# SyncE fetches the rows of the last two batches of each gather pass one by one, in a program without loops

## The chip, the cores and the metric

The kernel runs on one NeuronCore of a Trainium2 chip. The metric is device time in microseconds (us) from start to end of one execution, the median of the executions shown. A core has TensorE (PE; PEld is its weight load), VectorE (DVE), ScalarE (ACT), GpSimd (POOL) and SyncE (SP), each with an instruction stream of its own; they meet through semaphores. SyncE, ScalarE and GpSimd also issue DMAs, which 16 DMA engines carry out.

## What is computed

Four graph layers over 6250 nodes of 128 features and 106250 edges sorted by destination, each followed by a residual and a layernorm:

```
edge_index = stack([src, dst])
x = layernorm(x + L0(x))   # mean over a node's edges of x[src], then concat(x, mean) @ weight
x = layernorm(x + L1(x))   # segment max of relu([h[src], h[dst], w] @ W1 + b1) @ W2 + b2, then a two-layer update
x = layernorm(x + L2(x))   # gated convolution: sigmoid(gelu([x[row], x[col]] @ m1) @ m2) weighs xt[row]
x = layernorm(x + L3(x))   # attention with 4 heads: q[dst] . k[src], softmax over a node's edges, sum of v[src]
```

Every layer needs, for each edge, a row of a table at the edge's source node: `x[src]`, `h[src]` and so on. The number of the row is data, so the rows are gathered.

## The kernel before

Edges are padded to 832 tiles of 128 (`TILES`); four tiles are a batch of 512 edges (`BT`, `BE`), and a pass goes over 208 batches (`BATCHES`). Rows of a tile lie on the 128 partitions. There are four passes with gathers: `edges_sum` (L0, rows of 128 floats), `edges_max` (L1, 128), `edges_gate` (L2a, 192) and `edges_attention` (L3, 256). A fifth pass, `edges_conv` (L2), reads what L2a has put aside and gathers nothing. Between the passes `nodes` works on the nodes.

`gatherer` (L492) is GpSimd's program in a pass: for each batch it waits for a free buffer of eight (`room`, `DEEP`), counts up `s_go`, and issues four indirect DMAs of 128 rows each, whose row numbers stand in `g["src"]` (L503). It is written out without a loop. The other engines run `pipeline` (L63): rounds of 4 or 8 batches (`SLOTS`, `DEEP`) in a hardware loop, with the first and last rounds written out; a stage `(lag, f)` works on the batch that lies `lag` behind. Nothing plans the order: each engine's program is the order.

The data flow of L0: the gathered tiles are turned by TensorE into PSUM (`turn`, L567), VectorE runs a masked running sum over 512 edges (`scan`, L621, which needs the batch's mask), TensorE turns the sums back (L609), ScalarE copies them (L638) and stores them (L629). SyncE loads the masks (`mask_load`, L772, from the table `same`) into four slots, each when the scan four batches before is done, and stores zeros into `seed` (L385). In L1 SyncE loads a seed (L804) and two masks (L772) per batch; TensorE turns the seed (L818), VectorE spreads it over the edges (L855), adds the gathered row (`add_weight`, L846), adds the two (L861) and takes a running maximum (L868); ScalarE's relu and a matmul lie between. In L2a SyncE loads a seed (L925) and a mask (L929); VectorE's spread is L989. In L3 it loads a pair of rows (L1128) and a seed (L1132) per batch, and per four batches two masks (L1137), two rims (L1147) and a store (L1151). In all passes a buffer is given back to GpSimd by the stage that read it.

In a hardware loop, the address of a SyncE DMA follows from the loop's register, by a register operation and a move before the DMA instruction.

Of the kernel before, what the change touches and what calls it, by code (L numbers as in the profile page):

```python
# [13 lines left out]
P = 128  # L14
N, E, D = 6250, 106250, 128
HID = 64
# [11 lines left out]
NSLOTS = 3  # L28
COMBS = 7
# [33 lines left out]
def pipeline(eng, count, slots, stages, first=0):  # L63
# [4 lines left out]
    base, rounds = first // slots, count // slots  # L68
# [76 lines left out]
def build(nc, d, out):  # L145

    with ExitStack() as ctx:
# [12 lines left out]
        g["xT"] = sb("xT", [P, NT * P])  # L160
        g["last"] = sb("last", [P, NT], I32)
# [47 lines left out]
class Setup:  # L209
# [3 lines left out]
    def __init__(self, ph, d, g):  # L213
# [9 lines left out]
         self.s_rim, self.s_open) = (ph.sem(n) for n in ("src", "dst", "w", "x", "same", "id", "mask", "tp", "tc", "slink", "rim", "open"))  # L223
# [28 lines left out]
    def sync_first(self, sp):  # L252
        d, chunk = self.d, lambda a: a.rearrange("(p i) -> p i", p=P)
        sp.dma_start(self.g["src"][:, :], d["src"]).then_inc(self.s_src, 16)
        for j in range(3):
            sp.dma_start(self.dst[j][:, :], chunk(d["dst"][j:j + EP])).then_inc(self.s_dst, 16)
# [230 lines left out]
def edge_buffers(ph, width, depth=DEEP):  # L487
    gath = [ph.sb(f"gath{k}", [P, BT, width]) for k in range(depth)]
    return gath, ph.slot_sems("gath", depth), ph.sem("go")


def gatherer(gp, g, table, gath, s_gath, s_go, s_free, s_copied=None):  # L492

    depth = len(gath)
    for n in range(BATCHES):
        k, r = n % depth, n // depth
        if s_copied:
            stored(gp, s_copied, k, r)
        room(gp, s_free, n, depth)
        gp.sem_inc(s_go, 1)  # L500
        for t in range(BT):
            tile = n * BT + t
            gp.indirect_dma_start(out=gath[k][:, t, :], out_offset=None, in_=table,  # L503
                                  in_offset=bass.IndirectOffsetOnAxis(ap=g["src"][:, tile:tile + 1], axis=0)).then_inc(s_gath[k], 16)
# [17 lines left out]
def edges_sum(nc, d, g):  # L522

    with Phase(nc, "L0") as ph:
        gath, s_gath, s_go = edge_buffers(ph, D)
# [16 lines left out]
        @block.sync  # L542
        def _(sp):
            setup.sync_first(sp)
            beside.sync_before(sp)
            setup.sync_rows(sp)
            load, fill = mask_load(sp, g["same"], mask, s_mask, s_scan), beside.sync_stage(sp)
            pipeline(sp, BATCHES, SLOTS, [(0, load), (0, fill)])
            beside.all_filled(sp)
            setup.sync_last(sp)  # L550

        @block.gpsimd
        def _(gp):
# [3 lines left out]
            gatherer(gp, g, d["x"], gath, s_gath, s_go, s_turn)  # L557

        @block.tensor
        def _(pe):  # L560
            setup.tensor_first(pe, pX)

            def turn(n, k, r):
                landed(pe, s_gath, k, r, BT)
                room(pe, s_scan, n, 2)
                for t in range(BT):
                    m = pe.transpose(pT[k % 2][:, cols(t)], gath[k][:, t, :], g["ident"][:, :])  # L567
# [5 lines left out]
            for first, end, parts in stretches:  # L573
# [5 lines left out]
                pipeline(pe, end, DEEP, [(0, turn), (2, ret)], first=first)  # L579
# [196 lines left out]
def edges_max(nc, d, g):  # L776

    w = g["w"]
    with Phase(nc, "L1") as ph:
        gath, s_gath, s_go = edge_buffers(ph, D)  # L780
# [18 lines left out]
        def _(sp):  # L799
            sp.dma_start(weight[:, :], d["weight"]).then_inc(s_wt, 16)  # L800

            def load_seed(n, k, r):
                room(sp, s_turns, n, SLOTS)
                sp.dma_start(seed[k][:, :].rearrange("p (t f) -> p t f", t=BT), seeds[:, bass.ds(n * BT, BT), :]).then_inc(s_seed[k], 16)  # L804
            pipeline(sp, BATCHES, SLOTS, [(0, load_seed), (0, mask_load(sp, g["same"], same, s_same, s_dest)),
                                          (2, mask_load(sp, g["fresh"], fresh, s_fresh, s_max))])

        @block.gpsimd
        def _(gp):
            gatherer(gp, g, g["tab"], gath, s_gath, s_go, s_sent)  # L810
# [30 lines left out]
        def _(v):  # L841
            def add_weight(n, k, r):
                landed(v, s_gath, k, r, BT)
                room(v, s_turn, n, SLOTS)
                for t in range(BT):
                    a = v.scalar_tensor_tensor(sent[k % SLOTS][:, cols(t)], g["wide"]["W1w"][:, :], weight[:, bass.ds(n * BT + t, 1)],  # L846
                                               gath[k][:, t, :], ALU.mult, ALU.add)
# [22 lines left out]
            pipeline(v, BATCHES, DEEP, [(0, on_short(spread)), (0, add_weight), (1, on_short(add_dest)), (3, on_short(top))])  # L870
# [17 lines left out]
def edges_gate(nc, g, ew):  # L888
# [5 lines left out]
    with Phase(nc, "L2a") as ph:  # L894
        gath, s_gath, s_go = edge_buffers(ph, W2)
# [26 lines left out]
        def _(sp):  # L922
# [7 lines left out]
            pipeline(sp, BATCHES, SLOTS, [(0, load_seed), (0, load_same)])  # L930

        @block.gpsimd
        def _(gp):
            gp.iota(row_i[:, :], [[1, P]], base=0, channel_multiplier=0).then_inc(s_iota, 1)
            gatherer(gp, g, g["tab_h"], gath, s_gath, s_go, s_turn, s_aside)

        @block.tensor
        def _(pe):
            def turn(n, k, r):
# [7 lines left out]
                landed(pe, s_gath, k, r, BT)  # L947
                room(pe, s_pre, n, 2)
                pe.sem_inc(s_tgo, 1)
                for t in range(BT):  # L950
                    m = pe.transpose(pA[k % 2][H, cols(t)], gath[k][:, t, H], g["ident"][:, :])
# [17 lines left out]
            pipeline(pe, BATCHES, DEEP, [(0, turn), (2, dot), (9, count)])  # L969
# [68 lines left out]
        def _(act):  # L1038
# [5 lines left out]
            def put_aside(n, k, r):  # L1044
                landed(act, s_gath, k, r, BT)
                act.dma_start(aside[:, bass.ds(n * BT, BT), :], gath[k][:, :, HID:W2]).then_inc(s_aside[k], 16)
# [5 lines left out]
            pipeline(act, BATCHES, DEEP, [(0, put_aside), (0, on_short(gelu)), (4, on_groups(gate))])  # L1052
# [18 lines left out]
def edges_attention(nc, d, g):  # L1071
# [7 lines left out]
    with Phase(nc, "L3") as ph:  # L1079
        gath, s_gath, s_go = edge_buffers(ph, 2 * D)  # L1080
# [37 lines left out]
        def _(sp):  # L1118
# [33 lines left out]
            pipeline(sp, BATCHES, DEEP, [(0, on_short(load_pair)), (0, on_short(load_seed)), (0, on_groups(load_masks)), (12, on_groups(load_rims)), (19, on_groups(store_fix))])  # L1152
# [4 lines left out]
        def _(gp):  # L1157
# [7 lines left out]
            gatherer(gp, g, g["tab_kv"], gath, s_gath, s_go, s_pv)  # L1165
# [66 lines left out]
        def _(v):  # L1232
# [31 lines left out]
            def times_key(n, k, r):  # L1264
                need(v, s_query, n)
                landed(v, s_gath, k, r, BT)
                v.tensor_tensor(tiled(prod[k % 2][:, :]), tiled(pQ[k % 2][:, :]), gath[k][:, :, 0:D], ALU.mult).then_inc(s_prod, 1)
# [21 lines left out]
            def weigh(n, k, r):  # L1289
                need(v, s_probe, r * rings + k // SLOTS)  # L1290
                landed(v, s_gath, k, r, BT)
# [4 lines left out]
                                gath[k][:, :, D:2 * D].rearrange("p t (h c) -> p t h c", h=HEADS), ALU.mult).then_inc(s_pv, 1)  # L1296
# [544 lines left out]
```

## Time and profile before

| | |
|---|---|
| median of 3 runs (lowest, highest) | 6658.26 us (6647.23, 6663.53) |
| the profiled execution: its time, its span | 6670.73 us, 6669.0 us |
| granted TensorE clock, mean of the span | 0.64 |
| POOL, PE, DVE, ACT busy | 59%, 53%, 52%, 24% of the span |
| first to last gather of L0, L1, L2a, L3 | 5 to 1265, 1450 to 2826, 3028 to 4296, 5033 to 6502 us |

All views below are of that one execution. Times in them are microseconds from the span's start, durations of single instructions in a source view nanoseconds. "SPq" and "ACTq" are instructions of SyncE's and ScalarE's sequencers, DMA issues among them, which do not count as busy. In brackets stands how long the engine was idle before a row and what ended it: "issue" is nothing that the profile shows, "remote" a signal whose sender the profile doesn't name.

### The profile page before, as it was taken

What the parts mean: (1) busy time and instruction counts of PE and PEld (TensorE: products, weight loads), DVE (VectorE), ACT (ScalarE), POOL (GpSimd) and SP (SyncE); (2) the same over time, 40 slices, a digit from 0 to 9 for tenths busy, and PEclk for the clock granted to TensorE, in tenths of its full rate; (3) what the DMA queues carried; (4) which work ended last, traced back from release to release, by engine and by line L of the source; (5) the groups of instructions that cost most, each with busy time, mean ns of one, the idle gap of its engine ahead of it and who ended that gap; (6) DMA issues with size and microseconds to landing.
All of it is one profiled execution on the core that took longest, in us unless ns stands there. A gap on an engine that the chain in (4) does not pass through costs nothing. (4 is left out here: it accounts for less than half of the span.)

```text
span 6669.0 us, 85454 instructions
## 1 busy us (share of the span) xinstructions
PE 3561.5 (53%) x19032; PEld 2752.0 (41%) x19032; DVE 3479.4 (52%) x6921; ACT 1575.8 (24%) x3699; POOL 3955.5 (59%) x4526
## 2 busy tenths in 40 slices
PE   3433332245455555554667676766644676666661
PEld 2222222233333333333555555656633555555451
DVE  4444222225566666653666666778854444444445
ACT  1011000131111111131222222267740111111115
POOL 6666556655565655546666666488865555555552
PEclk6565565567777777775555555588876656666665
DMA  5555445424555555524555555489944555545552
GB/s 172 160 157 153 136 150 154 131 82 145 153 162 154 162 156 155 158 80 123 140 138 142 139 140 138 122 262 290 289 140 140 155 152 150 154 150 152 149 152 54
DMA packets 804105, 1015.40 MB, mean 152 GB/s; under 512 B 230791, under 2 KB 509457, under 8 KB 803988
## 3 DMA queue, kind: packets, MB, share of 16 engines
q1 hardware_dynamic: 454068, 466.36, 23.3%
q0 software_dynamic: 144320, 323.10, 18.7%
q10 hardware_dynamic: 205600, 224.71, 9.7%
q8 instruction: 33, 0.54, 0.0%
q14 instruction: 84, 0.69, 0.0%
HBM read 652.13 MB, written 361.61 MB: 152 GB/s over the span
## 5 line engine op out<-in xcount | busy, mean ns | idle before, releaser
L503 POOL DMA_INDIRECT L_gath<-tab_kv,src x832 | 787.4, 946 | 681.3 <-DVE L_pv L1294 428.1
L503 POOL DMA_INDIRECT L_gath<-tab,src x832 | 807.6, 971 | 572.0 <-DVE L_sent L846 324.7
L503 POOL DMA_INDIRECT L2a_gath<-tab_h,src x832 | 787.7, 947 | 481.0 <-issue 435.7
L503 POOL DMA_INDIRECT L_gath<-in_x,src x832 | 787.5, 947 | 475.4 <-issue 235.6
L638 ACT ACTIVATE L_back<-L_pB 128x512 f32<-128x512 f32 x624 | 365.6, 586 | 1386.7 <-remote 830.4
L621 DVE TENSOR_TENSOR_SCAN L_acc<-L_mask,L_acc,L_pT 128x512 f32<-128x512 bf16 x207 | 264.4, 1277 | 696.9 <-remote 640.0
L609 PE MATMUL L_pB<-ident,L_acc 128*128 128x128 f32 x2496 | 501.8, 338 | 232.0 <-issue 116.9
L609 PEld LDWEIGHTS L_pB<-ident,L_acc 128*128 128x128 f32 x2496 | 390.1, 178 | 412.7 <-issue 407.8
L1216 PE MATMUL L_pR<-L_pv,L_same 128*128 128x132 f32 x1664 | 375.4, 390 | 287.1 <-issue 130.6
L958 PE MATMUL L2a_pZ<-w_M,L2a_hid 64*128 64x1 f32 x1664 | 386.1, 350 | 244.1 <-DVE L2a_z L999 201.9
L958 PEld LDWEIGHTS L2a_pZ<-w_M,L2a_hid 64*128 64x128 f32 x1664 | 370.0, 325 | 344.2 <-issue 278.2
L698 POOL TENSOR_SCALAR L_hoth<-L_row,L_high,ew_sb 128x49 f32<-128x49 bf16 x832 | 441.8, 559 | 67.8 <-DVE L_part L740 65.5
L855 DVE TENSOR_TENSOR_SCAN L_dest<-L_same,L_dest,L_pS 128x512 f32<-128x512 bf16 x207 | 262.4, 1268 | 418.1 <-remote 377.5
L989 DVE TENSOR_TENSOR_SCAN L2a_dest<-L2a_same,L2a_dest,L2a_pS 64x512 f32<-64x512 bf16 x207 | 262.1, 1266 | 407.2 <-remote 361.6
L831 PE MATMUL L_pM<-L_hid,w_W 128*128 128x512 f32 x416 | 310.9, 838 | 280.5 <-issue 134.1
L1216 PEld LDWEIGHTS L_pR<-L_pv,L_same 128*128 128x128 f32 x1664 | 325.1, 285 | 320.3 <-issue 200.9
L825 PE MATMUL L_pA<-ident,L_sent 128*128 128x128 f32 x832 | 174.4, 347 | 411.1 <-DVE L_sent L846 352.6
L567 PE MATMUL L_pT<-ident,L_gath 128*128 128x128 f32 x832 | 195.2, 382 | 352.2 <-DVE L_acc L621 199.0
L1042 ACT ACTIVATE L2a_hid<-L2a_pre,m 64x512 f32<-64x512 f32 x208 | 150.1, 722 | 940.3 <-DVE L2a_pre L995 683.9
L1261 DVE TENSOR_TENSOR L_same<-L_pD,L_lane 128x512 f32<-128x512 f32 x208 | 143.2, 689 | 407.5 <-DMA L_low<-low 274.1
L877 ACT ACTIVATE L_hid<-L_pre,b 128x512 f32<-128x512 f32 x208 | 150.1, 722 | 861.2 <-DVE L_pre L861 579.6
L1181 PE MATMUL L_pQ<-L_seed,L_same 128*128 128x128 f32 x1664 | 345.6, 372 | 0.0
(286 smaller groups left out, 7599.6 us busy)
## 6 DMA issues: line engine op xcount, KB each, us to landing
run<-L_back ACTq DMA_DIRECT2D x416, 256.0 KB
L_seed<-seed SPq DMA_DIRECT2D x416, 256.0 KB
run<-L_back ACTq DMA_DIRECT2D x208, 264.0 KB
seed<-L_zeros SPq DMA_DIRECT2D x208, 256.0 KB
sent<-L2a_gath ACTq DMA_DIRECT2D x208, 256.0 KB
L_sent<-sent SPq DMA_DIRECT2D x208, 256.0 KB
run<-L_back SPq DMA_DIRECT2D x208, 256.0 KB
L_mask<-same SPq DMA_DIRECT2D x208, 128.0 KB
```

Of the source, the lines that this page charges most:

```text
L503: gp.indirect_dma_start(out=gath[k][:, t, :], out_offset=None, in_=table, in_offset=bass.IndirectOffsetOnAxis(ap=g["src"][:, tile:tile + 1 ...
L567: m = pe.transpose(pT[k % 2][:, cols(t)], gath[k][:, t, :], g["ident"][:, :])
L609: m = pe.transpose(pB[k % 2][:, cols(t)], acc[k][:, cols(t)], g["ident"][:, :])
L621: v.tensor_tensor_scan(acc[k][:, :], mask[k][:, :], pT[k % 2][:, :], start_of(acc, n, k), ALU.mult, ALU.add).then_inc(s_scan, 1)
L638: act.activation(rows(back[k][:, :, :]), pB[k % 2][:, :], ACT.Copy).then_inc(s_back, 1)
L698: a = gp.tensor_scalar(hot_high[k][:, t, :], row[:, :], high[:, tile:tile + 1], ew[:, tile:tile + 1], ALU.is_equal, ALU.mult)
L831: pe.matmul(pM[k % 2][:, :], w["W2"][:, :], hid[k][:, :], start=True, stop=True).then_inc(s_msg, 1)
L855: v.tensor_tensor_scan(dest[k][:, :], same[k][:, :], pS[k % 2][:, :], start_of(dest, n, k), ALU.mult, ALU.add).then_inc(s_dest, 1)
L958: m = pe.matmul(pZ[k % 2][:, t:t + 1], hid[k % SLOTS][:, cols(t)], w["M2"][:, :], start=True, stop=True)
L989: v.tensor_tensor_scan(dest[k][:, :], same[k][:, :], pS[k % 2][H, :], start_of(dest, n, k), ALU.mult, ALU.add).then_inc(s_dest, 1)
L1181: m = pe.matmul(pQ[k % 2][:, cols(t)], same[k][:, cols(t)], seed[h][:, cols(t)], start=True, stop=True)
L1216: m = pe.matmul(pR[half][:, at:at + W3], same[k][:, cols(t)], pv[k % 2][:, t, :], start=True, stop=True)
```

## The change

The last two batches (206 and 207, `FIRST` = 206) of each gather pass no longer come through GpSimd. They hold 778 real edges. A buffer of their own, `side`, takes them; its rows beyond tile 6 are first set to zero by GpSimd. `Rows.fetch` is a new stage at the end of each of SyncE's steps: in step n (n < 195, `SIDE_STEPS`) SyncE loads four row numbers from SBUF into registers and issues four DMAs of one row each. So that the partition and the tile of each row are constants, SyncE's `pipeline` in the four passes is replaced by `steps`, written out for all 208 batches (`on_ring` gives the old stages their slots). GpSimd gathers 206 batches. The stages that read gathered rows take `rows_in.at(n, k)` and wait with `rows_in.landed`; their pipelines write the last two batches out (`tail`).

```diff
+SIDE = 2
+FIRST = BATCHES - SIDE
+SIDE_ROWS = 4
+SIDE_RING = P // SIDE_ROWS
+SIDE_STEPS = -(-(E - FIRST * BE) // SIDE_ROWS)
...
-def pipeline(eng, count, slots, stages, first=0):
+def pipeline(eng, count, slots, stages, first=0, tail=0):
...
-    base, rounds = first // slots, count // slots
+    base, rounds = first // slots, (count - tail) // slots
...
+    def landed(self, eng, n, k, r):
+        if isinstance(n, int) and n >= FIRST:
+            for j in range(SLOTS):
+                eng.wait_ge(self.s_side[j], 16 * SIDE_ROWS * len(range(j, SIDE_STEPS, SLOTS)))
+        else:
+            landed(eng, self.s_gath, k, r, BT)
+
+    def gather(self, gp, g, s_free, s_copied=None):
+
+        whole = (E - FIRST * BE) // P
+        gp.memset(self.side[:, whole:, :], 0.0).then_inc(self.s_blank, 1)
+        for n in range(FIRST):
...
+    def fetch(self, sp):
+
+        sp.wait_ge(self.s_blank, 1)
+
+        def fetch(n, k, r):
+            if n >= SIDE_STEPS:
+                return
+            _, row = self.nc.values_load_multi_w_load_instructions(
+                self.src[k:k + 1, r * SIDE_ROWS:(r + 1) * SIDE_ROWS], engines=[mybir.EngineType.SP], min_val=0, max_val=N - 1,
+                skip_runtime_bounds_check_because="src holds numbers of nodes, as the reference's own indexing needs")
+            for i in range(SIDE_ROWS):
+                p = k * SIDE_ROWS + i
+                sp.dma_start(self.side[p:p + 1, r:r + 1, :], self.table[bass.ds(row[i], 1), :].unsqueeze(0)).then_inc(self.s_side[k % SLOTS], 16)
+        return fetch
...
-            pipeline(sp, BATCHES, SLOTS, [(0, load), (0, fill)])
+            sp.wait_ge(setup.s_side_src, 16)
+            steps(BATCHES, SIDE_RING, [(0, on_ring(load, SLOTS)), (0, on_ring(fill, SLOTS)), (0, rows_in.fetch(sp))])
```

Two places show how instructions move. SyncE in L0, before, one batch of four in the body of its loop:

```order
L772 ISA
L772 DMA L_mask<-same 128x512
L60 REGISTER_ALU
L385 ISA
L385 DMA seed<-L_zeros 128x512
```

SyncE in L0 with the change, the first rows of one step (an ISA is the operation that makes an address in registers; L821 and L393 are the old L772 and L385):

```order
L821 DMA L_mask<-same 128x512
L393 DMA seed<-L_zeros 128x512
L541 TENSOR_LOAD side_src
L546 ISA
L546 DMA L_side<-in_x 1x128
```

The last two rows come four times in a step; the loop's branch and its register arithmetic are gone. GpSimd in L0, before, from its last small work to the next pass:

```order
L371 MEMSET L_tri 49x49
L373 AFFINE_SELECT L_tri<-L_tri 49x49
L503 DMA L_gath<-in_x,src 128x128 x832
L116 UNCONDITIONAL_BRANCH
L117 ISA
```

The same place with the change:

```order
L379 MEMSET L_tri 49x49
L381 AFFINE_SELECT L_tri<-L_tri 49x49
L522 MEMSET L_side 128x256
L531 DMA L_gath<-in_x,src 128x128 x824
L121 UNCONDITIONAL_BRANCH
```

A memset stands ahead of the gathers, and eight gathers are gone.

## Rows read from the trace of the kernel before

**Rows 1.** The page's head.

```profile
span 6669.0 us, 85454 instructions
```

**Rows 2.** Passes: stretch, length, busy us PE, PEld, DVE, ACT, POOL, clock, DMA share, GB/s.

```profile
5.00:1265.00 1260.00, 442.23 (x2593) 336.88 (x2593) 445.79 (x480) 126.62 (x212) 787.06 (x832) 0.59 0.51 155
1450.00:2826.00 1376.00, 694.05 (x2824) 453.06 (x2822) 811.86 (x1403) 254.04 (x409) 807.31 (x832) 0.74 0.53 155
3028.00:4296.00 1268.00, 844.24 (x3977) 688.48 (x3978) 763.85 (x1433) 285.69 (x348) 787.39 (x832) 0.50 0.53 138
5033.00:6502.00 1469.00, 926.14 (x4152) 743.85 (x4153) 679.90 (x1553) 268.57 (x1050) 787.50 (x833) 0.63 0.50 151
```

**Rows 3.** GpSimd in order of time, L0: start, length, idle before it.

```profile
1240.82 0.94 POOL L503 DMA_INDIRECT L_gath<-in_x,src  x1 [4.56 <-remote]
1242.06 0.94 POOL L503 DMA_INDIRECT L_gath<-in_x,src  x1 [0.30 <-issue]
```

**Rows 4.** All engines in order of time, start of L1.

```profile
1464.36 1.10 PE L818 MATMUL L_pS<-ident,L_seed 128*128 128x128 f32 x8 [0.80 <-ACT xT L882]
...
1474.69 0.33 SPq L804 DMA_DIRECT2D L_seed<-seed  x1
1474.69 1.28 DVE L855 TENSOR_TENSOR_SCAN L_dest<-L_same,L_dest,L_pS 128x512 f32<-128x512 bf16 x1 [5.46 <-remote]
```

**Rows 5.** By line, SyncE and ScalarE: min/median/max ns, first and last start.

```profile
L772 SPq FUSED_REGOPS  x199: 3/46/732, 60.9 to 1257.8; - x199
L772 SPq MOVE L_mask<-same x199: 3/29/1352, 61.0 to 1258.5; - x199
...
L1128 SPq DMA_DIRECT2D L_pair<-dst x204: 3/243/1111, 5046.0 to 6479.8; - x102
...
L629 ACTq DMA_DIRECT2D run<-L_back x198: 338/343/577, 61.3 to 1262.1; - x198
```

**Rows 6.** SyncE's loads in order of time, late in L0.

```profile
1224.45 0.71 SPq L772 DMA_DIRECT2D L_mask<-same  x1
1228.00 0.69 SPq L385 DMA_DIRECT2D seed<-L_zeros  x1
...
1241.50 0.34 SPq L772 DMA_DIRECT2D L_mask<-same  x1
1242.03 0.35 SPq L385 DMA_DIRECT2D seed<-L_zeros  x1
```

**Rows 7.** SyncE's waits in 60:1265, 1466:2826, 3033:4296, 5044:6502: us, times, longest.

```profile
SPq L772 <- DVE L_acc L621: 286.5, 69, 26.0
...
SPq L772 <- DVE L_acc L868: 309.4, 93, 18.6
...
SPq L925 <- remote: 425.6, 62, 29.8
SPq L929 <- DVE L2a_dest L989: 164.5, 100, 4.1
...
SPq L1132 <- DMA L_sent<-sent: 363.9, 58, 11.6
SPq L1132 <- PE L_pQ L1181: 236.7, 58, 8.9
```

**Rows 8.** VectorE after the last gathers of L0, L1 and L2a.

```profile
1269.38 8.30 DVE L621 TENSOR_TENSOR_SCAN L_acc<-L_mask,L_acc,L_pT 128x512 f32<-128x512 bf16 x6 [15.14 <-remote]
...
2840.24 1.25 DVE L855 TENSOR_TENSOR_SCAN L_dest<-L_same,L_dest,L_pS 128x512 f32<-128x512 bf16 x1
2844.23 1.25 DVE L855 TENSOR_TENSOR_SCAN L_dest<-L_same,L_dest,L_pS 128x512 f32<-128x512 bf16 x1
...
4298.23 1.26 DVE L989 TENSOR_TENSOR_SCAN L2a_dest<-L2a_same,L2a_dest,L2a_pS 64x512 f32<-64x512 bf16 x1
4301.94 1.26 DVE L989 TENSOR_TENSOR_SCAN L2a_dest<-L2a_same,L2a_dest,L2a_pS 64x512 f32<-64x512 bf16 x1
```

**Rows 9.** DMA issues: count, us to landing.

```profile
N_got<-run,last POOLq DMA_INDIRECT x196, 2.5
```

More of the change, by code:

```diff
@@ L222, in __init__ @@
         (self.s_src, self.s_dst, self.s_w, self.s_x, self.s_same, self.s_id, self.s_mask, self.s_tp, self.s_tc, self.s_link,
-         self.s_rim, self.s_open) = (ph.sem(n) for n in ("src", "dst", "w", "x", "same", "id", "mask", "tp", "tc", "slink", "rim", "open"))
+         self.s_rim, self.s_open, self.s_side_src) = (ph.sem(n) for n in ("src", "dst", "w", "x", "same", "id", "mask", "tp", "tc", "slink", "rim", "open", "sidesrc"))
         w, wide = g["w"], g["wide"]
@@ L484, in vector_after, with __init__, at @@
         link(v.tensor_copy(g["first"][:, :], a[:, :]))
[L487 to L504, printed above, removed]
+class Rows:
+    def __init__(self, nc, ph, g, table, width, depth=DEEP):
+        self.nc, self.src, self.table, self.depth = nc, g["side_src"], table, depth
+        self.ring = [ph.sb(f"gath{k}", [P, BT, width]) for k in range(depth)]
+        self.side = ph.sb("side", [P, SIDE * BT, width])
+        self.s_gath, self.s_go, self.s_blank = ph.slot_sems("gath", depth), ph.sem("go"), ph.sem("blank")
+        self.s_side = ph.slot_sems("side", SLOTS)
+    def at(self, n, k):
+        if isinstance(n, int) and n >= FIRST:
+            return self.side[:, (n - FIRST) * BT:(n - FIRST + 1) * BT, :]
+        return self.ring[k][:, :, :]
+    def landed(self, eng, n, k, r):
+        if isinstance(n, int) and n >= FIRST:
+            for j in range(SLOTS):
[6 more added lines that the diff above has]
+        for n in range(FIRST):
+            k, r = n % self.depth, n // self.depth
+            if s_copied:
+                stored(gp, s_copied, k, r)
+            room(gp, s_free, n, self.depth)
+            gp.sem_inc(self.s_go, 1)
+            for t in range(BT):
+                tile = n * BT + t
+                gp.indirect_dma_start(out=self.ring[k][:, t, :], out_offset=None, in_=self.table,
+                                      in_offset=bass.IndirectOffsetOnAxis(ap=g["src"][:, tile:tile + 1], axis=0)).then_inc(self.s_gath[k], 16)
+    def fetch(self, sp):
[10 more added lines that the diff above has]
+        return fetch
@@ L507, in short, with on_ring @@
+def on_ring(f, slots):
+    return lambda n, k, r: f(n, k % slots, r * (SIDE_RING // slots) + k // slots)
 def short(k, r):
@@ L578, in _ @@
                     m.then_inc(s_own, 1)
-                pipeline(pe, end, DEEP, [(0, turn), (2, ret)], first=first)
+                pipeline(pe, end, DEEP, [(0, turn), (2, ret)], first=first, tail=SIDE if end == BATCHES else 0)
         @block.vector
```

60 lines of the change are left out of this document (32 added, 28 removed).

## The prediction

> **What bounds the kernel now.** I read the page's head first, then the stretches, then each queue in the order of time. The profiled execution spans 6669.0 us [rows 1], and its own time is 6670.73, 12.5 us above the median 6658.26; I sum against the former and carry the difference over.
>
> Four passes over 208 batches of four gathers take most of it: 1260, 1376, 1268 and 1469 us from first gather to last [rows 2]. GpSimd works through a gather in 0.94 us and starts the next 0.30 us later [rows 3], so a batch costs it 4 x 1.247 = 4.99 us and a pass 1037. The passes run at 6.05, 6.61, 6.10 and 7.06 us a batch. The difference, 1.1 to 2.1 us, is GpSimd standing before a buffer that isn't free, 4.56 us in one case [rows 3]. So GpSimd is the first bound, not the only one. The DMA engines are half used in the gather passes [rows 2].
>
> Why do buffers come free late? Signals arrive late while gathers stream. At the start of L1, TensorE's eight transposes of two seed batches end at 1465.46; VectorE's second scan and SyncE's next seed load, which both wait for the second batch, start together at 1474.69 [rows 4], 9.2 us later. No engine shown is busy with anything they need. I call such stretches crowded.
>
> SyncE suffers in them too, and it alone. In L0 its register operations have a median of 0.046 and 0.029 us but maxima of 0.73 and 1.35, while ScalarE's DMA issue in the same pass hardly moves, 0.338 to 0.577 [rows 5]. Two SyncE loads that belong together stand 3.55 us apart when it is crowded and 0.53 when it isn't [rows 6]. Each such load is three instructions in the trace (two register operations, the issue).
>
> How much room has SyncE? Its recorded waits are 286.5 us in L0, 309.4 in L1, 425.6 + 164.5 in L2a, 363.9 + 236.7 in L3 [rows 7], of windows of 1205, 1360, 1263 and 1458 us with 199, 200, 201 and 204 batches. The rest is occupied: **4.6, 5.25, 3.35 and 4.2 us a batch**, for 2, 3, 2 and about 3.25 loads. It is free for only 1.4 to 3.0 us of each.
>
> **The change, part by part.** *Removed:* eight of 832 gathers per pass. At 1.247 us each that is 10.0 us of GpSimd, but the end of a pass is not its last gather. After it, VectorE still works through queued batches without a gap: six scans in 8.30 us in L0, 1.4 a batch; 4.0 a batch in L1; 3.7 in L2a [rows 8]. The two side batches must still be worked through. What goes is two batches at the pass's pace, less two at the tail's: 2 x (6.05 - 1.4) = 9.3, 2 x (6.61 - 4.0) = 5.2, 2 x (6.10 - 3.7) = 4.8. L3's tail isn't listed by batch; with L2a's 3.7 it is 6.7. Sum **-26 us**. The bound is the full pace, 2 x 25.8 = -52.
>
> *Added on SyncE:* 195 of 208 steps get a register load of four numbers and four one-row DMAs, each with a register operation and, as for every DMA addressed by a register before, a move. That is 13 instructions a step. The old loads lose theirs, since their places are constants: two or three instructions stay where six or nine stood (each with loop arithmetic). In L0 the step goes from about 6 instructions to 15.
>
> Price of a step, uncrowded: an old load 0.45 (0.53 less the register part); a row DMA 0.42, since the smallest load listed, two rows, takes 0.243 to issue against 0.35 [rows 5] and the spacing is otherwise that of the 0.53 pair. The register load has no row. Its lower bound is a register operation, 0.046 [rows 5]; the upper one is a transfer from issue to landing, 2.5 [rows 9]. I take 0.7: it returns data to the sequencer, so it is more than a register operation, but nothing crosses a DMA queue, and it lies nearest to a stretched register operation (0.73 [rows 5]). The Trainium skill, page "DMA: Bandwidth & Descriptors", section "Latency and other measured facts", gives tensor_load a floor of about 600 ns; no run yet shows it, and by it the step would be 0.1 us cheaper. Together F = 0.9 + 0.7 + 1.7 = 3.3 us in L0, 3.7 in L1, L2a and L3 alike within 0.2.
>
> Crowded: 3.55 / 3 = 1.2 us per instruction, C = 15 x 1.2 = 18 us in L0, 19 in L1.
>
> How much of a batch is crowded? A step before was 1.06 us free and 7.1 crowded in L0 (two spacings); a mean of 4.6 makes 59% of steps crowded, 0.59 x 7.1 = 4.2 us of each 6.05. The same sum gives 4.3 us in L1 (1.6, 10.7, mean 5.25), 2.6 in L2a (1.2, 7.1, 3.35) and 3.1 in L3 (1.5, 11.5, 4.2).
>
> If crowding c goes with the gathers' streaming, it stays the same per batch, and a SyncE that never rests needs T = c + F x (1 - c/C) a batch:
> L0: 4.2 + 3.3 x 0.77 = 6.73, against 6.05, +0.68 x 195 = **+132**.
> L1: 4.3 + 3.7 x 0.77 = 7.2, against 6.61, **+117**.
> L2a: 2.6 + 3.5 x 0.86 = 5.6, under 6.10, **0**. L3: 3.1 + 3.7 x 0.84 = 6.2, under 7.06, **0**.
> With the register load at 0.046 the two sums are 6.2 and 6.7, +52 in all; at 2.5 all four passes go over, 8.1, 8.6, 7.1 and 7.7, about +1120.
>
> Who waits: the masks and seeds stand behind the row DMAs on SyncE. A late mask holds VectorE's scan, then TensorE's PSUM buffer, then GpSimd's room for the next gather. With four slots SyncE can't work ahead.
>
> *Nothing or nearly:* two memset tiles a pass (about 0.5 us, GpSimd, before its first gather), one more small load at the start, one more unrolled round on the other engines (their waits cover it), and the DMA engines' share: 780 rows of 512 or 1024 bytes, 0.4 to 0.8 MB a pass beside some 200. A rule against the change: the same page's "Rules for kernel authors" says to coalesce many small transfers. Taken as one after another with the fixed 2 us that the page gives, 780 would be 1560 us a pass, more than any pass. The loads that follow each other in 0.53 us [rows 6] show issue overlapping what comes after it, so my sum uses the spacing.
>
> Sum: -26 + 132 + 117 = **+223 us**, 6892 of span, **6880 us** against the median.
>
> **Rivals.**
> *SyncE keeps up, faster.* If waits that the profile doesn't list (for a zero fill to land, for instance) make up much of the 3.55 us spacing, or the crowding eases as soon as GpSimd pauses, SyncE needs only F = 3.3 to 3.7 us a step, well inside 6.05 to 7.06. Then the four tails' -26 to -52 stand: 6606 to 6632 us. It decides by one number: SyncE's step under T. For it: medians of 0.03 to 0.05 us. Against it: 4.6 us a batch already spent in L0 on two loads.
> *Half of each.* L0 and L1 lose a tenth of a microsecond a batch, 2 x 195 x 0.1 = 39, and the tails give 26 back: about +13, no change that can be measured.
> *Runaway.* The register load must itself wait its turn in a crowded stretch (2.5 us or more): +1120 less 26, 7750 us, with L2a and L3 late as well.
> *The change doesn't relieve GpSimd at all:* were all four passes paced by late signals alone, the tails' gain would be 0 and everything rests on SyncE. It is inside the second case.
>
> **How the numbers follow.** Something above 0.3% (20 us) is what a measurement here can tell from no change. My forecast, SyncE bound in one or more passes, gets 0.52, the runaway 0.08; SyncE keeping up 0.24; half of each 0.16. The range takes in the faster case from 6620 and the slow one to 7300, well past the middle of the way to the runaway; about 1 in 10 lies beyond each end or less.
>
> **What would show it.** Right: SyncE without waits of note in L0 and L1, the spacing of its old loads above 6.05 us, GpSimd's idle time before gathers up by over 200 us in the two passes, and L2a and L3 near 1268 and 1469 less 12. Register loads of 0.5 to 1 us. Wrong: SyncE's waits for VectorE still there, passes 8 to 13 us shorter each. Runaway: register loads of several microseconds and all passes longer. The mean of SyncE's instructions in L2a against L0 tells whether crowding follows the gathers or SyncE's own traffic.

## The result, and the profile after

The changed kernel takes 6720.09 us (median of four runs, 6714.07 to 6722.85) against 6660.9 us for the kernel before, measured beside it: a ratio of 1.0091, with a 95% interval of 1.0073 to 1.0108. That is 59 us slower. The forecast was 6880, 222 us above the median of before that it started from, so the direction is right and the size is not. The time lies inside the range of 6620 to 7300.

The head of the page (compare [rows 1]) shows 5055 instructions more. The rise is the row fetches (13 instructions in each of 4 x 195 steps are 10140), less the register and loop instructions that SyncE no longer needs:

```profile
span 6715.9 us, 90509 instructions
```

The stretches of the four passes, columns as in [rows 2]:

```profile
6.00:1300.00 1294.00, 464.94 (x2576) 346.17 (x2577) 448.57 (x479) 126.03 (x211) 779.17 (x824) 0.55 0.49 149
1481.00:2837.00 1356.00, 702.93 (x2796) 460.67 (x2794) 804.23 (x1390) 252.93 (x406) 812.10 (x824) 0.72 0.55 156
3047.00:4322.00 1275.00, 842.15 (x3950) 676.82 (x3951) 763.01 (x1420) 282.80 (x344) 779.92 (x824) 0.50 0.52 137
5063.00:6536.00 1473.00, 918.48 (x4090) 738.10 (x4091) 669.25 (x1521) 263.33 (x1030) 778.52 (x824) 0.63 0.50 149
```

GpSimd issues 824 gathers a pass instead of 832, and three of the four passes are longer all the same. The exact starts come from the gather line, as first and last start in each pass:

```profile
L531 POOL DMA_INDIRECT L_gath<-in_x,src x824: 938/944/1697, 5.6 to 1299.3; - x165
L531 POOL DMA_INDIRECT L_gath<-tab,src x824: 938/944/1517, 1480.9 to 2836.3; - x165
L531 POOL DMA_INDIRECT L2a_gath<-tab_h,src x824: 940/946/1484, 3046.8 to 4321.0; - x165
L531 POOL DMA_INDIRECT L_gath<-tab_kv,src x824: 940/946/1080, 5062.5 to 6534.9; - x165
```

From these, and the same line of the kernel before, the whole difference of 47 us between the two spans can be laid out. A pass is counted from its first gather's start to its last one's, a gap from there to the next pass, the last gap to the end of the span.

| | L0 | L1 | L2a | L3 | sum |
|---|---|---|---|---|---|
| pass before | 1259.2 | 1375.4 | 1267.2 | 1467.4 | 5369 |
| pass after | 1293.7 | 1355.4 | 1274.2 | 1472.4 | 5396 |
| of the difference: two batches fewer at the old pace | -12.1 | -13.2 | -12.2 | -14.1 | -52 |
| of the difference: pace of the other 206 | +46.6 | -6.8 | +19.2 | +19.1 | +78 |
| us a batch, before | 6.05 | 6.61 | 6.09 | 7.06 | |
| us a batch, after | 6.28 | 6.58 | 6.19 | 7.15 | |
| gap behind the pass, after less before | -3.8 | +7.6 | +3.5 | +12.8 | +20 |

So L0 pays most, L1 pays nothing, and L2a and L3, for which I had forecast no price, pay 19 us each.

SyncE's waits in the four passes of the changed kernel, the longest entries of each (us, times, longest):

```profile
SPq L821 <- DVE L_acc L670: 13.7, 3, 7.6
...
SPq L821 <- DVE L_acc L917: 37.9, 26, 8.1
...
SPq L978 <- DVE L2a_dest L1038: 15.3, 25, 3.8
...
SPq L1181 <- DMA run<-L_back: 58.2, 24, 10.2
SPq L1181 <- PE L_pQ L1231: 21.5, 19, 4.4
```

All its recorded waits come to 17, 44, 19 and 95 us in the four passes. Before they were 287, 347, 660 and 622 us, some small entries more than [rows 7] lists. So the waits have nearly gone in all four passes, not in two: SyncE is occupied almost without a break. VectorE's scan of L0 now names what it lacks. This is the idle time before it, with the longest cause:

```profile
its engine sat idle before it (us, times) until:
  DMA L_mask<-same: 400.7, 80
```

Before, 640.0 of the scan's 719 us of idle time ended with a signal of unnamed sender, so how much of the lateness of masks is new can't be read; the idle time grew by 85 us in all. In the order of SyncE's program the mask's load stands behind the row DMAs, as the prediction's chain had it. Two excerpts of the same 55 us of L0 show how the price arises. GpSimd in order of time:

```profile
999.17 0.94 POOL L531 DMA_INDIRECT L_gath<-in_x,src  x1 [0.30 <-issue]
...
1019.28 0.94 POOL L531 DMA_INDIRECT L_gath<-in_x,src  x1 [19.18 <-PE L_pT L616]
1021.92 0.94 POOL L531 DMA_INDIRECT L_gath<-in_x,src  x1 [1.69 <-issue]
```

SyncE in order of time, the four row DMAs of a step together in one line:

```profile
1009.41 1.56 SPq L546 DMA_DIRECT2D L_side<-in_x  x4
1011.03 0.35 SPq L821 DMA_DIRECT2D L_mask<-same  x1
1011.43 0.42 SPq L393 DMA_DIRECT2D seed<-L_zeros  x1
1012.92 1.56 SPq L546 DMA_DIRECT2D L_side<-in_x  x4
...
1016.07 1.56 SPq L546 DMA_DIRECT2D L_side<-in_x  x4
...
1024.78 0.26 SPq L821 DMA_DIRECT2D L_mask<-same  x1
...
1034.10 0.69 SPq L821 DMA_DIRECT2D L_mask<-same  x1
1034.79 0.02 SPq L393 DMA_DIRECT2D seed<-L_zeros  x1
1039.01 12.61 SPq L546 DMA_DIRECT2D L_side<-in_x  x4
1052.32 0.69 SPq L821 DMA_DIRECT2D L_mask<-same  x1
```

While GpSimd stands, from 1000 to 1019, SyncE makes a step every 3.15 to 3.5 us. While the gathers stream, from 1022 on, one step takes 9.3 us (mask load to mask load, 1024.78 to 1034.10) and the next 18.2 (to 1052.32), its four row DMAs alone 12.61. GpSimd runs ahead by its eight buffers, SyncE falls behind, GpSimd has to stop for 19 us, and in that pause SyncE catches up.

The excerpt shows an extreme, not the rule. Taken over all 189 steps of L0 that fetch, from mask load to mask load, the median is 5.5 us, nine in ten stay within 11.4, and 18.22 is the longest. The 14 steps in which GpSimd starts no gather take 2.7 to 3.8 us, median 3.16. The 69 steps in which the gathers never pause take 3.2 to 18.2 us, median 6.75, mean 7.6.

### The profile page after: what moved, and what is told of

The parts are those of the page before. It is cut to its first block and busy times, and to the rows that moved or that the text cites. A ratio compares the mean times of both kernels' runs of the same rounds, so it can differ in the third digit from the quotient of the medians.

```text
span 6715.9 us, 90509 instructions
## 1 busy us (share of the span) xinstructions
PE 3599.5 (54%) x19032; PEld 2761.7 (41%) x19032; DVE 3491.5 (52%) x6921; ACT 1577.0 (23%) x3699; POOL 3937.7 (59%) x4498
## 3 DMA queue, kind: packets, MB, share of 16 engines
q0 software_dynamic: 143040, 320.22, 18.2%
## 5 line engine op out<-in xcount | busy, mean ns | idle before, releaser
L670 DVE TENSOR_TENSOR_SCAN L_acc<-L_mask,L_acc,L_pT 128x512 f32<-128x512 bf16 x207 | 264.9, 1280 | 779.4 <-DMA L_mask<-same 400.7
L616 PEld LDWEIGHTS L_pT<-ident,L_gath 128*128 128x128 f32 x824 | 139.8, 206 | 675.0 <-issue 652.7
L994 PE MATMUL L2a_pS<-ident,L2a_seed 128*64 128x128 f32 x832 | 218.3, 416 | 288.7 <-DMA L2a_seed<-seed 261.9
```

Of the source, the lines that this page charges most:

```text
L616: m = pe.transpose(pT[k % 2][:, cols(t)], rows_in.at(n, k)[:, t, :], g["ident"][:, :])
L670: v.tensor_tensor_scan(acc[k][:, :], mask[k][:, :], pT[k % 2][:, :], start_of(acc, n, k), ALU.mult, ALU.add).then_inc(s_scan, 1)
L994: m = pe.transpose(pS[k % 2][H, cols(t)], seed[h][:, t * HID:(t + 1) * HID], g["ident"][:, :])
```

## The experiments

One fact first, without which the numbers can't be read. The kernels ran in five groups, each beside the kernel before on one chip. That same kernel took 5291 us beside e1 to e4 and 5295 beside e5 and e6, but 6647 beside e7 and e8, 6671 beside e9 to e12 and 6595 beside e13 to e15. I call these the 5290 level and the 6650 level; the forecast and its result belong to the latter, and so do all statements on late signals and stretched instructions. Chip 1 gave both (e5, e6 and e13 to e15), so the level doesn't belong to the chip. What sets it is not known. Each ratio is against the kernel before of the same group, with a 95% interval. Differences between kernels of two groups go by these ratios, and carry the intervals of both.

### At the 5290 level

**e1, SyncE written out and nothing else.** Starting from the changed kernel, the fetch stage is taken out of the four written-out programs and GpSimd gathers everything:

```
-        for n in range(FIRST):
+        for n in range(BATCHES):
-            steps(BATCHES, SIDE_RING, [(0, on_ring(load, SLOTS)), (0, on_ring(fill, SLOTS)), (0, rows_in.fetch(sp))])
+            steps(BATCHES, SIDE_RING, [(0, on_ring(load, SLOTS)), (0, on_ring(fill, SLOTS))])
```

> SyncE's program of the changed kernel, written out for all four passes, but without the row fetches; GpSimd gathers all 208 batches, as before. Theory A (the loss is SyncE's: it carries 13 further instructions per step, and in the changed kernel it waits for only 17, 45, 19 and 97 us in the four passes, where it waited for 314, 347, 659 and 622 before): without the fetches SyncE waits again by hundreds of us in each pass, and the time is that of before, 6660 within 15. Theory C (the written-out program and the peeled last batches cost by themselves): a good part of the +59 is still there, over 6690.

Measured: 5295.05 us, ratio 1.0004 (0.9995 to 1.0013). Theory C falls at this level. Its test where the change loses is e12.

**e2, the last two batches left out.** No fetch; the side tiles are zeros.

> Leaves out the rows of the last two batches (zeros in their place): GpSimd gathers 206 batches, SyncE's program is written out and fetches nothing. This is the gain that the change could have had at most. My term of the sum was 26 us; from the two traces the changed kernel's tails and passes give 31 (two batches at the paces of before, 52 us, less 21 us by which the stretches between the passes grew). Both theories: 6660 less 26 to 31, so about 6632; if the last batches' work runs as fast as everything behind the gathers allows, as low as 6608.

Measured: 5273.7 us, ratio 0.9967 (0.9955 to 0.9979), a gain of 17.6 us, or 21 against e1: less than the 26 to 31 I expected, and less than the change itself gains here (e5).

**e3, fetch and gather all.**

```
         if isinstance(n, int) and n >= FIRST:
             for j in range(SLOTS):
                 eng.wait_ge(self.s_side[j], ...)
-        else:
-            landed(eng, self.s_gath, k, r, BT)
+        landed(eng, self.s_gath, k, r, BT)
```

> SyncE fetches the 778 rows as in the changed kernel, but GpSimd gathers all 208 batches and these are used; the fetched rows are waited for and then unused. This is the price of the fetch alone. Theory A and theory B (the row transfers crowd the gathers' transfers): both give the changed kernel's paces of 6.28, 6.58, 6.19 and 7.15 us for two more batches in each pass, about 6745. If the price were bound up with what the side batches do at the end, it would be nearer to 6690.

Measured: 5285.42 us, ratio 0.9991 (0.9982 to 1.0). The whole fetch costs nothing here; the kernel is even 10 us faster than e1, which gathers the same and fetches nothing. My number was for the other level, and both theories missed. At the 6650 level this kernel was not run.

**e4 and e6, the fetch on ScalarE.** SyncE gets its loop back, ScalarE's four programs are written out, and `fetch` goes into them:

```
-            pipeline(act, BATCHES, SLOTS, [(2, copy_rows(...)), (2, store_rows(...))])
+            steps(BATCHES, SIDE_RING, [(2, on_ring(copy_rows(...), SLOTS)), (2, on_ring(store_rows(...), SLOTS)),
+                                       (0, rows_in.fetch(act))])
```

> The same fetch of the same rows (register load, address arithmetic, 4 row transfers a step), issued by ScalarE in place of SyncE in all four passes; ScalarE's program is written out, SyncE's is the loop of before. Theory A: ScalarE's instructions are not stretched in the trace (30 to 50 ns for register work, 0.35 us for a DMA issue, so about 2.5 us a step on an engine that is busy 10 to 20% of its time), the passes go back to 6.06 to 7.07 us a batch, and the time is 6625 to 6650, below both kernels. Theory B (the transfers themselves are what costs): the same 6700 to 6720 as the changed kernel. If ScalarE's own work is what the fetch delays (its copies free PSUM and buffers late), it comes out above 6720.

> The fetch on ScalarE in all four passes, once more, beside the change itself. Where before takes about 5291 us: 5272 as measured, level with the change within 5. Where it takes about 6661 us, theory A (SyncE's stretched instructions): 6625 to 6650, below both kernels; theory B (the row transfers crowd the gathers): 6700 to 6720, as the changed kernel; if ScalarE's own copies come late through it, above 6720.

Measured: 5272.11 us, ratio 0.9963 (0.9949 to 0.9976), and 5269.0 us, ratio 0.9948 (0.9935 to 0.9962). The first expectation was for the other level; the second, level with the change within 5 us, held (5267.75 beside it, e5). At this level it doesn't matter who fetches.

**e5, the change itself.**

> The changed kernel itself, unedited, beside the kernel before. The four runs so far fell where the kernel before takes 5291 us instead of 6661: there GpSimd's own work paces all four passes (5.03 us a batch) and late signals are gone. Theory A (late signals are what stretches SyncE's instructions): where before takes about 5291 us the change is a gain, 5291 less 15 to 20, 5272 to 5278; where it takes about 6661 us the change is again a loss of 40 to 75 us. Theory D (written out, the fetch costs SyncE the same everywhere): a loss of 40 us or more in both.

Measured: 5267.75 us, ratio 0.9948 (0.9935 to 0.9962): here the change is a **gain of 26.8 us**. Theory D falls. Theory A has the direction, but the gain is larger than its 15 to 20 us. The stretches of its four passes, columns as in [rows 2]:

```profile
5.00:1036.00 1031.00, 454.56 (x2610) 365.60 (x2611) 454.79 (x484) 129.11 (x216) 779.57 (x824) 0.55 0.61 192
1179.00:2216.00 1037.00, 674.68 (x2880) 435.50 (x2878) 832.89 (x1431) 252.74 (x418) 785.69 (x824) 0.84 0.74 208
2370.00:3401.00 1031.00, 869.77 (x4045) 672.31 (x4044) 787.40 (x1462) 292.85 (x356) 780.00 (x824) 0.50 0.66 171
4100.00:5131.00 1031.00, 826.05 (x4119) 667.53 (x4120) 681.24 (x1540) 274.62 (x1037) 780.05 (x825) 0.73 0.71 214
```

All four passes run at 5.00 to 5.03 us a batch, the 4.99 us that the prediction worked out for GpSimd alone. So the rest, 1.1 to 2.1 us a batch at the other level, is lateness and not GpSimd's work. Nor are the DMA engines busy for longer there: DMA share times length gives 634, 746, 663 and 737 us in the four passes of the changed kernel at the 6650 level, and 629, 767, 680 and 732 here. The granted clock isn't it either: in L2a it is 0.50, the 1.2 GHz level, in both, at 6.19 and 5.00 us a batch. The same lines of SyncE at the two levels show it too (min/median/max ns). Of the changed kernel at the 6650 level:

```profile
L541 SPq TENSOR_LOAD <-side_src x780: 3/502/1547, 29.2 to 6451.5; - x195
...
L546 SPq FUSED_REGOPS  x3120: 2/37/1431, 29.8 to 6453.7; - x195
L546 SPq MOVE L_side<-in_x x780: 2/29/1420, 29.9 to 1288.7; - x195
L546 SPq DMA_DIRECT2D L_side<-in_x x780: 2/250/1409, 30.0 to 1288.8; - x195
```

and of e5, where no register operation is stretched:

```profile
L541 SPq TENSOR_LOAD <-side_src x780: 472/502/1507, 29.2 to 5058.3; - x195
...
L546 SPq FUSED_REGOPS  x3120: 37/37/51, 29.8 to 5060.2; - x195
L546 SPq MOVE L_side<-in_x x780: 29/29/38, 29.9 to 970.6; - x195
L546 SPq DMA_DIRECT2D L_side<-in_x x780: 224/250/918, 29.9 to 970.6; - x195
```

### At the 6650 level

**e7, every row fetched twice.**

```
-            for i in range(SIDE_ROWS):
+            for to, i in [(to, i) for to in (self.side, self.spare) for i in range(SIDE_ROWS)]:
                 p = k * SIDE_ROWS + i
-                sp.dma_start(self.side[...
+                sp.dma_start(to[...
```

> SyncE fetches every one of the 778 rows twice, the second time into a spare tile that nothing reads. This looks for the point from which SyncE decides. Theory A, where before takes about 5290 us: per step one register load of 0.53 to 0.88 us and 8 rows at 0.08 + 0.06 + 0.35 us, with two to three old loads at 0.4 to 0.5 us, is 5.5 to 5.8 us of SyncE in 195 steps of each pass, against 5.0 us of GpSimd: 95 to 150 us more per pass, together about 5750 (5600 to 5850), and SyncE's waits gone. If a row costs SyncE nothing while its transfer runs, 5270 as the change. Where before takes about 6660 us: every pass over 7.3 us a batch, above 7000.

Measured: 7196.93 us, ratio 1.0817 (1.0791 to 1.0843). The paces are 6.98, 6.78, 6.96 and 7.79 us a batch; "over 7.3 in every pass" held in L3 alone, "above 7000" held. In L0 the second 780 rows cost (6.98 - 6.28) x 206 = 144 us. The first cost 62 (against the 5.98 of e12, below): the price per row is rising.

**e8, three batches aside, SyncE and ScalarE in turn.**

```
-SIDE = 2
+SIDE = 3
         def fetch(n, k, r):
+            n = 2 * n + turn
+            k, r = n % SIDE_RING, n // SIDE_RING
```

> Three batches aside in place of two (1290 rows, 323 steps), the steps taken in turn by SyncE and ScalarE, so each carries 162 in place of 195. Where before takes about 5290 us, both engines have room and each batch taken from GpSimd is worth its 5.0 us less what it costs behind the gathers, 26.8/8 = 3.3 us as the change measured: 12 x 3.3 = 40, so 5254. If the batch behind the gathers costs as much as it saves, 5268, as the change. Where before takes about 6660 us: SyncE is still stretched, 6660 to 6700.

Measured: 6824.89 us, ratio 1.0269 (1.0248 to 1.0289). That is 125 us above the range I expected. The paces are 6.28, 6.73, 6.45 and 7.26 us a batch. It is the first sign that ScalarE is no refuge.

**e11, the fetch on ScalarE, as in e4.**

> The fetch on ScalarE in all passes. Where before takes about 6650 us: in e8 ScalarE's fetch instructions were stretched too, if less than SyncE's (register work 0.2 us in place of 0.06, SyncE's 0.33), and L2a lost 155 us of GpSimd's time to ScalarE's late stores. Theory A: L0, L1 and L3 come near the paces of before, L2a stays at 6.4, 6670 to 6700. Theory B (rows cost whoever fetches): 6720 or more. Both engines' copies late: above 6750. Where before takes about 5290 us: 5270.

Measured: 6813.57 us, ratio 1.0219 (1.0196 to 1.0241): more than twice the loss of the change, and by the expectation's three cases the last (above 6750). SyncE keeps its loop here, so its paces stand against those of before and not of e12. The row lines read as SyncE's did. The first is the register work of all passes; its maximum is 1.40 us, where e5's was 0.05:

```profile
L546 ACTq FUSED_REGOPS  x3120: 2/37/1404, 56.9 to 6545.6; - x195
...
L546 ACTq DMA_DIRECT2D L_side<-in_x x780: 2/235/1409, 57.1 to 1288.4; - x195
```

The worst pass is L2a, at 6.50 us a batch. There GpSimd waits, before it may reuse a buffer, until ScalarE has put its second half aside (GpSimd's waits between 3000 and 4380 us):

```profile
POOL L2a_gath L531 <- DMA sent<-L2a_gath: 232.0, 72, 6.8
```

In the kernel before this wait was 20.1 us in L2a, 21 times. ScalarE's stores stand behind its row DMAs, and GpSimd pays. L0, at 6.26, is as slow as with SyncE's fetch.

**e12, as e1.**

> SyncE written out, no fetch, all 208 batches gathered. Where before takes about 6650 us: within 15 of before. If SyncE's fewer instructions (no register work for the loads) let its loads go out earlier and the passes follow, up to 40 us less. If it is slower, by fetching more program, up to 30 us more. Where before takes about 5290 us: 5290 to 5295.

Measured: 6631.26 us, ratio 0.9941 (0.9925 to 0.9958), a **gain of about 40 us** from writing the loads out. The passes are 1243.6, 1365.2, 1256.5 and 1458.3 us, 46 us less than before in all. SyncE's waits in L0 and L2a (stretches of 1244 and 1257 us):

```profile
SPq L819 <- DVE L_acc L668: 678.9, 78, 28.3
...
SPq L972 <- remote: 458.2, 50, 30.0
SPq L976 <- DVE L2a_dest L1036: 233.2, 115, 4.2
SPq L972 <- PE L2a_pS L992: 130.4, 29, 10.7
```

In L0 SyncE is occupied for (1244 - 679) / 208 = 2.7 us a batch, where it was 4.6. In L2a it is 2.1. The 3.35 of before leaves out a third entry, which e12's figure has in it:

```profile
SPq L925 <- PE L2a_pS L945: 69.4, 18, 8.8
```

With it L2a was at 3.0. Counted the same way, with all recorded waits, L1 falls from 5.1 to 3.0 and L3 from 4.1 to 2.7. The same loads leave in both kernels; only the register and loop instructions between them are gone.

What that does to two loads that belong together shows in the order of time. In the kernel before, 199 such pairs in L0 start 0.53 to 6.30 us apart, median 1.52; 3.55 was the pair of [rows 6]. In e12 the median of 201 pairs is 0.36, and 187 lie within 0.5. Two of them, while gathers stream every 1.25 us:

```profile
519.02 0.32 SPq L819 DMA_DIRECT2D L_mask<-same  x1
519.38 0.43 SPq L393 DMA_DIRECT2D seed<-L_zeros  x1
526.56 0.32 SPq L819 DMA_DIRECT2D L_mask<-same  x1
526.93 0.43 SPq L393 DMA_DIRECT2D seed<-L_zeros  x1
```

So streaming gathers alone don't stretch SyncE's DMA issues: with nothing between the two loads, they leave close together at the 6650 level too.

**e9, as e2.**

> As e2 (rows of the last two batches left out, nothing fetched, SyncE's program written out). Where before takes about 6650 us: the gain of the removal alone, two batches at 6.1 to 7.1 us in each pass, 52 us, less what they cost behind the gathers (20 us by the gaps of the changed kernel): 6650 less 30, about 6620 (6600 to 6630). Then the fetch's own price is the changed kernel's +59 plus this, about 90 us. Where before takes about 5290 us: 5274 as in e2.

Measured: 6602.62 us, ratio 0.9895 (0.9864 to 0.9925), 69 us less than before. The removal alone, e9 against e12, is 29 us in the medians, with an uncertainty of some 20 (e9's four runs lie between 6587 and 6627): the passes lose 48, the gaps behind them grow by 24.

**e10, constant rows.**

```
-            _, row = self.nc.values_load_multi_w_load_instructions(self.src[...], ...)
             for i in range(SIDE_ROWS):
-                p = k * SIDE_ROWS + i
-                sp.dma_start(self.side[p:p + 1, r:r + 1, :], self.table[bass.ds(row[i], 1), :]...
+                p, row = k * SIDE_ROWS + i, (n * SIDE_ROWS + i) * 2311 % N
+                sp.dma_start(self.side[p:p + 1, r:r + 1, :], self.table[row:row + 1, :]...
```

> The change with row numbers that are constants: the same 195 x 4 row transfers a pass from SyncE's queue, but of rows that are not the edges' (the last two batches get wrong rows), without register load, address arithmetic and moves: 4 instructions more a step in place of 13. Where before takes about 6650 us: theory A (SyncE's stretched instructions cost): SyncE waits again in L0 and L1, and the time is near that of e9, 6620 to 6650. Theory B (the row transfers and their signals cost): 6700 to 6720. Where before takes about 5290 us: 5268 by both.

Measured: 6644.28 us, ratio 0.996 (0.9943 to 0.9977). Theory A had the number, and SyncE waits again, 411.5 us for the scan in L0. The 3120 row transfers together with the 3120 instructions that issue them cost 42 us (e10 less e9, again with some 20 either way). The register load, address work and moves cost the rest, about 87 us: the change stands at +60 by its ratio, e10 at -27. With e15's ratio for the change, +48, it is 75. Address work isn't all of it, though: with four plain issues more in each step, 66 of L0's 200 pairs of loads are over 0.5 us apart again, against 14 of 201 in e12. What is not tested is whether it matters that e10's rows are others.

**e13, one row a step.**

```
-            for i in range(SIDE_ROWS):
+            for i in range(1):
```

> The change with one row transfer a step in place of four (three of four side rows stay zero): register load, one address operation, one move, one transfer, so 4 further instructions a step, as many as e10 with its four transfers of constant rows. Where before takes about 6660 us: theory A (SyncE's instructions are the price) gives what e10 gave, 0.996 of before, 6635 to 6650; theory B (the transfers and their signals are) gives a quarter of e10's distance to e9, 6610 to 6620. Where before takes about 5290 us: 5268 by both.

Measured: 6554.67 us beside 6594.81, ratio 0.9943 (0.9929 to 0.9957). This doesn't decide. As written, on 6660 us, it is 6622, next to theory B's 6620. By ratios, B's quarter of the way from e9 to e10 would be 0.9911 and A's value 0.996, and the measurement is two thirds of the way to A, with an interval that overlaps e10's and falls just short of e9's. The effect I wanted to split is 0.65% in all, too small for a comparison across groups. Within its own group e13 says this much: three rows of four less, with their address work, are worth 86 us against the change (e15).

**e14, one batch aside.**

```
-SIDE = 2
+SIDE = 1
```

> One batch aside in place of two: 266 rows, 67 steps with a fetch in each pass. Where before takes about 6660 us: written out alone 0.994 (-40 us), removal of one batch a pass -14, and a third of the fetch's price of 130 us, +43: 6650 if the price goes with the rows, 6615 to 6630 if SyncE has room for so few. Where before takes about 5290 us: half of the change's gain, 5281.

Measured: 6544.28 us beside 6594.81, ratio 0.992 (0.9906 to 0.9933). As written, on 6660 us, that is 6607, below both of the expected cases. With 67 fetching steps in a pass the price is nearly nil: against e12's 0.9941 the gain grows by about the 14 us that the removed batch is worth (the two intervals overlap). This is a complete kernel that is faster than both, by 50 us than before and by 97 us than the change, all in one group. At the 5290 level it wasn't tried.

**e15, the change again.**

> The changed kernel beside these two, for a direct comparison. Where before takes about 6660 us: 1.009 of it, 6720. Where before takes about 5290 us: 0.995, 5268.

Measured: 6641.07 us, ratio 1.0072 (1.0058 to 1.0085). The loss is there in a second group, at 46 us a little smaller than the 59 of the first.

| at the 6650 level | ratio | L0 | L1 | L2a | L3 (us a batch) |
|---|---|---|---|---|---|
| before | 1 | 6.05 | 6.61 | 6.09 | 7.06 |
| e12, written out only | 0.9941 | 5.98 | 6.56 | 6.04 | 7.01 |
| e9, and two batches left out | 0.9895 | 5.99 | 6.59 | 6.05 | 6.97 |
| e10, and four constant rows a step | 0.9960 | 6.09 | 6.64 | 6.10 | 7.08 |
| the change, rows by number | 1.0091 | 6.28 | 6.58 | 6.19 | 7.15 |
| e11, by ScalarE | 1.0219 | 6.26 | 6.62 | 6.50 | 7.20 |
| e13, one row a step | 0.9943 | 5.96 | 6.45 | 6.06 | 6.90 |
| e14, one batch aside | 0.9920 | 5.99 | 6.40 | 6.02 | 6.96 |
| e15, the change | 1.0072 | 6.16 | 6.41 | 6.09 | 7.04 |

The last three rows are one group, in which L1 ran faster in all three kernels. Within it the change again pays most in L0 and nothing in L1.

## Why the prediction was right in direction and wrong in size

**The tails, -26: right.** The table gives -51.6 for the batches at the passes' pace and +20.1 for the gaps, -31 in all; e9 against e12 gives -29. The 26.8 us that the change gained at the 5290 level are no confirmation: with a pace of 5.0 us in every pass the prediction's own sum, two batches at the pace less two at the tail's, is only -15.

**The written-out program, taken at nothing: wrong, -40.** The prediction said that the old loads lose their register instructions and used it only to count a step's 15. It never asked what those instructions were costing. SyncE's occupancy of 4.6 us a batch was read as two loads; in e12 1.9 us of it went with the loop and address work. The writing out is worth 0.05 to 0.07 us a batch in each pass.

**The price of an uncrowded step, 3.3 us: right.** With GpSimd standing the median is 3.16 us. The register load has a median of 0.502 us (0.7 taken). The floor of about 600 ns that the Trainium skill, page "DMA: Bandwidth & Descriptors", section "Latency and other measured facts", gives for tensor_load is a little above that median; the measured 0.502 decides.

**The crowded price of a step, 18 us, and the crowded time per batch, 4.2, 4.3, 2.6 and 3.1 us: this is the step that failed.** The prediction took one pair of old loads, 3.55 us apart, as 1.2 us for any of SyncE's instructions while gathers stream, got 18 us for a step of L0 from it, mixed free and crowded steps until the old occupancy came out, and held the crowded time so found fixed. Three things that the runs show stand against it. The 18 us are the longest of 189 steps; with gathers streaming throughout, a step takes 7.6 us on average. The 3.55 us belonged to loads with address work between them; without it, at the same level, the pair takes 0.36 (e12). And the old occupancy from which the mixture was worked out was in part work that the change removed (e12), while in L2a lateness hid in waits of 425.6 us for an unnamed source [rows 7].

What came of it, in the prediction's own terms: the price of the fetch was forecast as 132, 117, 0 and 0 us, 249 in all. Against e12's paces it was 62, 3, 30 and 28, about 125. With the -40 of the writing out and the -29 of the removed batches that makes +56, against +59 measured. So of the 163 us by which the forecast was too high, 40 are the writing out, and some 125 the fetch's price. (L1's 117 is in part rounding: its own terms give 0.55 x 195 = 108.)

The formula isn't mended by one number. With 7.6 for 18 it gives 4.2 + 3.3 x (1 - 4.2/7.6) = 5.7 us in L0, under the old pace. With the 18 kept, the measured paces ask for a crowded time of 3.6 in L0, 3.6 in L1, 3.3 in L2a and 4.3 in L3, less than forecast in two passes and more in two. The direction is right because the fetch's price, though half of the forecast, is still more than the 69 us that the writing out and the removed batches give back.

**The chain from late masks to GpSimd: it fits L0.** 400.7 us of the scan's idle time end with the mask's landing. GpSimd's wait for TensorE before L0's gathers grew from 63.7 to 132.4 us, but its waits with unnamed sender fell from 173.3 to 139.1, so 35 us are new, as much as the pass is longer. The forecast of over 200 us more idle time in two passes fell with the sum.

**The rival "SyncE keeps up"** is what happens at the 5290 level. That the gain there has its number, 26.8 us against the -26 of its lower end, is luck, as said above. At the 6650 level part of its condition holds: crowding eases as soon as GpSimd pauses, at 1000 to 1019 us of the changed kernel. That limits the loss without removing it, since GpSimd must stand for it. **Runaway** fell: the register load stays at half a microsecond in the median (1.547 at most). The rule of the Trainium skill that the prediction cites, to coalesce small transfers (page "DMA: Bandwidth & Descriptors", section "Rules for kernel authors"), points the right way here, but not at the 2 us a transfer with which the prediction tried it: 3120 of them cost 42 us with their issuing (e10 less e9), or 13 ns each.

**Instructions or transfers.** Counted over the ratio of e9, the fetch costs about 32 us in e13 (3120 instructions more on SyncE, 780 transfers), 43 in e10 (3120 and 3120), and 118 to 130 in the change (10140 and 3120). That is 10 to 14 ns for each added instruction in all three, while e10 and the change have equal numbers of transfers and differ threefold in price. So the number of instructions on SyncE is the better account of these three. e14 doesn't fit it: 3484 instructions at almost no price, in the first third of each pass. These are comparisons across groups, and a smaller price of the transfers themselves can't be told from none.

**That SyncE suffers alone** was wrong: ScalarE's fetch instructions are stretched as far as SyncE's (1.40 us at most in e11, 1.43 in the change).

What stays open: why L1 pays nothing with three loads a step, why e14 pays almost nothing, and what the fetch alone, with all batches gathered as in e3, costs at the 6650 level. Nor did any run show what makes the instructions late at one level and not at the other.

## What to carry to other kernels

Before work is put on a queue that has waits, find out what the queue's occupied time is made of, and take its loop and address work out first; that alone was worth 0.6% here at the 6650 level and nothing at the other, and a third of the added work then fitted at almost no price. A queue's waits measured with today's instructions are no budget for others if the time of an instruction depends on what a neighbour is doing: price a step once while the neighbour runs and once while it stands, and take the spread of many steps, not one excerpt. A gain or loss of under 1% should be measured at more than one time, since the same change was -0.5% at one level of the machine and +0.9% at another.

## What the runs showed that I had not expected

- The same kernel, on the same chip, took 5295 us in one group of runs and 6595 in another. At the faster level each gather pass runs at GpSimd's 5.0 us a batch, and the stretched instructions and late signals are absent (maximum of a register operation of the row fetches 51 ns against 1431).
- ScalarE, whose instructions stayed within 0.577 us in [rows 5], is stretched like SyncE (register operations up to 1.40 us) as soon as it fetches rows itself (e11). That its queue had looked undisturbed said only that it had little to issue.
- The first 67 batches of L0 run at 6.00 us a batch before and 6.08 after, but batches 67 to 195 at 6.14 and 6.42. The loss in L0 sits almost wholly in the later part, though the fetch is the same in both.
